# The order of the quantising steps carried on into steps 48 to 55, and one norm's rstd moved ahead on GpSimd

## The reference

```
x = x + tanh(g_xattn[0]) * xattn0(layernorm(x), ctx)
x = x + tanh(g_ffn[0])   * ffn0(layernorm(x))        # MX: fp6 activations, fp4 weights
x = x + tanh(g_xattn[1]) * xattn1(layernorm(x), ctx)
x = x + tanh(g_ffn[1])   * ffn1(layernorm(x))        # int4 weights, a permutation, a bias

xattn: 32 query heads, 8 KV heads of 128; q and k are RMS-normalised per head;
       softmax(q k^T / sqrt(128) + mask) v, then the output projection
ffn0:  mxlinear(silu(mxlinear(x, w_gate)) * mxlinear(x, w_up), w_down)
mxlinear(x, w): both are rounded to a low-bit float in blocks of 32 with a shared exponent
```

## Time and profile before

| | us |
|---|---|
| median of 3 runs | 1346.63 |
| lowest, highest | 1345.92, 1347.79 |
| profiled execution, its own time | 1346.49 |
| its span | 1344.6 |

### The profile page before, as it was taken

The page is one execution under the profiler, slowest core; times in us unless marked ns, Lnnn a source line. Parts: engine busy times, 40 slices in busy tenths (PEclk is TensorE's granted clock), DMA queues, the critical chain, the costliest instruction groups (busy, mean ns, idle before and its releaser), DMA issues.

```text
span 1344.6 us, 25713 instructions
## 1 busy us (share of the span) xinstructions
PE 1336.9 (99%) x7841; PEld 1135.6 (84%) x7841; DVE 960.4 (71%) x1984; ACT 837.0 (62%) x3299; POOL 635.2 (47%) x682
## 2 busy tenths in 40 slices
PE   9999999999999999999999999999999999999999
PEld 7888888888888888777777788888888888888887
DVE  6878787887878798788888857766555555555656
ACT  6767676676767675556656556655666656565542
POOL 3456556564646575356767424432434333332232
PEclk9999999999999999999999999999999999999999
DMA  8011212102121210010100022001010100100001
GB/s 291 1 60 50 67 50 65 52 22 64 49 66 49 67 50 21 1 48 32 49 32 1 1 79 79 32 1 56 32 47 31 45 33 0 47 31 1 2 8 56
DMA packets 32957, 59.49 MB, mean 44 GB/s; under 512 B 2928, under 2 KB 24304, under 8 KB 28784
## 3 DMA queue, kind: packets, MB, share of 16 engines
q1 hardware_dynamic: 32592, 58.01, 13.0%
q10 hardware_dynamic: 288, 0.52, 0.1%
HBM read 56.43 MB, written 2.10 MB: 44 GB/s over the span
## 4 chain that ended last, share of the span: by engine, by line
PE 96%; DVE 1%; POOL 1%; issue 1%; DMA 0%; ACT 0%; SPq 0%; POOLq 0%; DVEq 0%; ACTq 0%
PE bank L1210 66%; PE bank L1202 9%; PE bank L1274 8%; PE bank L1301 7%; PE bank L1236 3%; PE bank L1395 1%; PE bank L1291 1%; PE bank L1407 1%; DMA w_raw<-in_wv 0%; DVE w_lo L823 0%; PE bank L1382 0%; POOL probs L560 0%; POOL rstd L523 0%; DVE probs L1046 0%; POOL f_s L513 0%
## 5 line engine op out<-in xcount | busy, mean ns | idle before, releaser
L494 POOL TENSOR_TENSOR w_lo<-w_raw,w_hi (+1 forms) x150 | 210.7, 1420 | 174.9 <-ACT w_hi L661 174.9
L694 ACT ACTIVATE squares<-bank 128x128 bf16<-128x128 f32 x512 | 134.4, 278 | 196.3 <-PE bank L1210 196.3
L1046 DVE SCALAR_TENSOR_TENSOR probs<-bank,mask_sb 128x512 f32<-128x512 f32 x127 | 87.6, 690 | 205.6 <-PE bank L1274 190.8
L642 ACT ACTIVATE probs<-probs,negmax 128x128 f32<-128x128 f32 x512 | 198.4, 392 | 7.0 <-DVE negmax L929 4.5
L519 POOL TENSOR_TENSOR meansq<-sumsq,scalars 128x5 f32<-128x5 f32 x128 | 28.1, 219 | 359.1 <-ACT squares L694 359.1
L523 POOL TENSOR_TENSOR rstd<-meansq,scalars 128x5 f32<-128x5 f32 x128 | 153.1, 1196 | 10.8 <-POOL meansq L519 1.1
L1210 PE MATMUL bank<-w_hi,oT_hi 128*128 (+1 forms) x512 | 151.1, 417 | 0.0
L1210 PE MATMUL bank<-w_hi,xT_hi 128*128 (+1 forms) x512 | 141.1, 396 | 0.0
L1210 PE MATMUL bank<-w_lo,oT_hi 128*128 (+1 forms) x512 | 138.1, 391 | 0.0
L1210 PE MATMUL bank<-w_hi,oT_lo 128*128 (+1 forms) x512 | 137.9, 391 | 0.0
L1210 PE MATMUL bank<-w_lo,xT_hi 128*128 (+1 forms) x512 | 137.6, 390 | 0.1
(11 more groups left out here) (143 smaller groups left out, 3058.7 us busy)
## 6 DMA issues: line engine op xcount, KB each, us to landing
w_raw<-in_wq SPq DMA_DIRECT2D x16, 1024.0 KB, 4.9
w_raw<-in_wo SPq DMA_DIRECT2D x16, 1024.0 KB, 4.8
fw_raw<-in_ffn_w SPq DMA_DIRECT2D x36, 192.0 KB, 2.3
w_raw<-in_wk SPq DMA_DIRECT2D x16, 256.0 KB, 5.3
w_raw<-in_wv SPq DMA_DIRECT2D x16, 256.0 KB, 5.4
x_sb<-in_x SPq DMA_DIRECT2D x7, 256.0 KB, 9.6
ctx_raw<-in_ctxT SPq DMA_DIRECT2D x7, 256.0 KB, 9.1
fw_raw<-in_ffn_w SPq DMA_DIRECT2D x7, 256.0 KB, 2.7
```

The source lines that it names most:

```text
L494: last = nc.gpsimd.tensor_tensor(lo, raw, hi.bitcast(FP32), ALU.subtract)
L642: last = nc.scalar.activation(probs[:, h * P:(h + 1) * P], probs[:, h * P:(h + 1) * P], ACT.Exp, bias=negmax[:, h:h + 1], accum_out=rowsum ...
L694: last = nc.scalar.activation(squares[:, h // 2, (b + 1) % 4, h % 2, :], q_bank(n, kind)[:, h * P:(h + 1) * P], ACT.Square, scale=SCALE, a ...
L1046: nc.vector.scalar_tensor_tensor(heads(probs[:, :]), heads(psSQ[:, :]), SCALE, mask_sb[:, :].unsqueeze(1).to_broadcast([P, REP, P]), ALU.m ...
```

## The change

A function `calm(n, kind)` is true in QUANT steps and in ZONE steps below 56. Where the order asked for `kind == QUANT`, it now asks for `calm`, on ScalarE, DVE and PE. So steps 48 to 55 take the QUANT order of exponentials, kT, inverse, scores, masked scores and their followers. The place of the weight split isn't touched: it still goes by the kind, on ScalarE (`split_upper`) and GpSimd (`split_lower`). Step 56 has both exponentials now, as step 48 had. On GpSimd, the rstd of the first feed-forward norm (tile 0, in step 56 alone) stands ahead of `unit_rstd`, not behind it.

```diff
+        def calm(n, kind):
+            return kind == QUANT or (kind == ZONE and n < FFN0)
+        def qn_first(n, kind, t):
+            return kind == FIRST or calm(n, kind) or t.down is not None or t.next is not None
...
@@ GpSimd, step
                     split_lower(split_pieces(n, b, kind, j))
+                if t.norm == 0:
+                    ln_rstd_of(NORM["ffn", t.norm])
...
                 if has(n, 0):
                     unit_rstd(n)
...
-                if t.norm is not None:
+                if t.norm is not None and t.norm:
                     ln_rstd_of(NORM["ffn", t.norm])
@@ ScalarE, step
-                exp_late = exp_after(kind) or (kind == FIRST and b == BATCHES - 1)
+                exp_late = calm(n, kind) or (kind == FIRST and b == BATCHES - 1)
...
-                if exp_after(kind) or (kind == ZONE and n == ZONE0):
+                if calm(n, kind) or (kind == ZONE and n == FFN0):
                     softmax_exp(n - 1)
                 if kind in (ZONE, PLAIN):
                     split_upper(split_pieces(n, b, kind, j))
...
-                    if t.active or kind == QUANT:
+                    if t.active or calm(n, kind):
                         layer = layer_of(n, 0, kind)
                         act.wait_ge(kt_ps, n + 1)
                         nc.scalar.activation(kT[:, :], psKV[:, 2 * P:3 * P], ACT.Copy,
@@ VectorE, step
-                    if kind != QUANT:
+                    if not calm(n, kind):
                         row_inverse(n)
...
-                if kind == QUANT:
+                if has(n, 2) and calm(n, kind):
                     row_inverse(n)
...
-                if has(n, 1) and not qn_first(kind, t):
+                if has(n, 1) and not qn_first(n, kind, t):
                     maximum(n)
-                if has(n, 2) and (t.gate is not None or kind == QUANT):
+                if has(n, 2) and (t.gate is not None or calm(n, kind)):
                     probs_lower(n)
                 if has(n, 0) and kind != FIRST:
                     scaled_q(n, kind, t)
...
-                if has(n, 1) and qn_first(kind, t):
+                if has(n, 1) and qn_first(n, kind, t):
                     maximum(n)
...
-                if has(n, 0) and not t.active and kind != QUANT:
+                if has(n, 0) and not t.active and not calm(n, kind):
@@ PE, step
-                if kind == QUANT:
+                if calm(n, kind):
                     scores()
                 if has(n, 2):
                     probabilities()
-                if has(n, 1) and kind != QUANT:
+                if has(n, 1) and not calm(n, kind):
                     scores()
```

More of the change, by code:

```diff
@@ L1054, in step @@
                     scaled_q(n, kind, t)
-                if has(n, 2) and qn_first(kind, t) and kind != QUANT:
+                if has(n, 2) and qn_first(n, kind, t) and not calm(n, kind):
                     probs_lower(n)
-                if has(n, 1) and qn_first(kind, t):
+                if has(n, 1) and qn_first(n, kind, t):
                     maximum(n)
-                if has(n, 2) and t.gate is None and not qn_first(kind, t):
+                if has(n, 2) and t.gate is None and not qn_first(n, kind, t):
                     probs_lower(n)
```

## The result

The changed kernel takes 1349.05 us (median of 19 runs, 1348.70 to 1350.78), the kernel before 1346.78 (19 runs): a ratio of 1.0018, 95% interval 1.0011 to 1.0025. It is slower by 0.18%, or 2.3 us. The forecast was 1349.3 and 0.2%.

The account below looks back on a forecast made before the run. PE was taken to bound the kernel, with a floor of 9.53 us per step without feed-forward work. The terms -0.72 + 5 x 0.82 - 0.67 = +2.7 us gave 1349.3 against the median of 1346.63; range 1344.0 to 1352.0.

Parts of the forecast that it names:

- Step 48: In the new order it takes 9.53 us, like a QUANT step, instead of 10.25: -0.72.
- Steps 49 to 53: Later w_lo on GpSimd holds DVE's scaling, PE's load stalls 1.02: each step 10.55 instead of 9.73, price 0.82.
- Step 57: Earlier rstd brings f_s about 0.9 us earlier, PE's wait goes, the step is as long as step 59: -0.67.
- rival A: New order works as in QUANT steps: steps 49 to 53 fall to 9.53, sum -2.4 us, 1344.2; chance 0.18.
- B: Rival: GpSimd's rstd holds DVE as well in steps 49 to 53, 2.53 each: +11.3 us, 1357.9; chance 0.06.
- C: Rival: stall comes, but step 48's 0.72 turns up in step 56, step 57 gains nothing: +4.1, 1350.7; chance 0.08.

Follow-up runs that it names:

- one w_lo late: Changed kernel with the second w_lo of steps 49, 50, 52 and 53 put last on GpSimd: 1346.20 us, ratio 0.9993.
- the last experiment: Changed kernel with the weight split also in its QUANT place below step 56, first six pieces a step earlier: 1345.10 us, ratio to the kernel before 0.9984.
- the order alone: Changed kernel with GpSimd's rstd of norm 0 back behind the unit's: 1351.35 us, ratio 1.0031.

## Why the prediction was right

**Step 48: right.** -0.72 forecast, -0.72 measured.

**Steps 49 to 53: right in mechanism and nearly in size.** In step 50, counted from its start, forecast and measured: w_hi starts 2.23 and 2.24, v_hi 3.52 and 3.53, the last w_lo ends 5.71 and 5.65, masked scores 7.37 and 7.32, scaled q 8.58 and 8.52, PE's load 9.31 and 9.25, the step 10.55 and 10.44. So the price was 0.71 in four steps, not 0.82. 0.06 of the difference is the shorter pair of w_lo (2.71 in the trace), the other 0.05 lies behind PE's load, where I had let the rest of the step take 1.24 and it takes 1.19. In step 49 the price was 1.17. The piece of step 48 has four blocks, and its last GpSimd instruction ends later:

```profile
472.62 1.05 POOL L537 TENSOR_TENSOR fw_out<-fw_y,blk_pow 128x512 bf16<-128x512 f32 x1
473.70 0.71 DVE L879 STREAM_TRANSPOSE fw_turned<-fw_out 128x512 bf16<-128x512 bf16 x1 [1.66 <-POOL fw_out L537]
...
475.26 2.97 POOL L494 TENSOR_TENSOR w_lo<-w_raw,w_hi 128x512 fp32r<-128x512 f32 x2 [1.60 <-ACT w_hi L663]
...
475.57 1.53 DVE L1019 TENSOR_TENSOR probs<-probs,rinv 128x512 f32<-128x512 f32 x1
```

So DVE came to L1019 0.31 behind w_lo and not 0.36 ahead of it, and was held by it. The second w_lo ended 5.90 into the step instead of 5.65, and it held L857 instead of L860, so that the two 12-column instructions behind L857 were still to come:

```profile
477.23 1.04 DVE L857 TENSOR_SCALAR amax<-amax 128x12 f32<-128x12 f32 x1
```

I had taken the five steps as alike. That DVE came late because of the fourth block is read from the trace, and no run tests it; that the held L1019 costs about 0.48 is what step 49 with one w_lo late shows. The two errors nearly cancel by luck: 3.99 against 4.1.

The forecast read a QUANT step off step 47, which has no piece. Nothing went wrong by it: step 45, which has one of three blocks, also takes 9.53, and step 48 of the changed kernel does too.

**Step 57: right in sign, -0.85 where I took -0.67** as the most there was. I had bounded it by step 59, which takes in a down product's result as well (L999 on DVE); step 57 without its stall is 13.04, shorter than that. Whether that extra work is the 0.18 between them is not shown. The bound was wrong, not the mechanism: L513, L889 and the transposes did what was forecast.

**The time.** The forecast sum was +2.7 and the steps give +2.42: 0.11 less from steps 49 to 53, 0.18 less from step 57. That the medians differ by 2.3 is worth less as support, since the stated range, 1344.0 to 1352.0, took in no change and rival A as well. The positions inside the steps decide.

**Rival A** (-2.4) named what the order could give if nothing collided, and the last experiment shows it (-2.43 in the stretch), with the split moved too. **B** is refuted: in step 50 rstd runs from 489.12 to 490.68, and L866 runs inside it in its usual 0.36. The Trainium skill, "SBUF — State Buffer", section "Who interferes with whom", has whoever issues first, GpSimd or a DVE instruction in a two-port mode, keep the shared pair of ports for the whole instruction. The trace agrees for the 1.28 us of a w_lo. It disagrees for a 5-column rstd, if L866 is in such a mode; no view names the mode. **C** is refuted: step 56 takes 9.52.

## What to carry to other kernels

When a block of instructions is moved to another place in an engine's order, list what else is issued relative to it: here the exponentials moved, w_hi stood behind them, w_lo behind w_hi, and so w_lo began 1.5 us later in the step, on top of the piece's scaling, though no line of GpSimd's in these steps was touched. Where DVE and GpSimd keep each other out, what to look at is where the last long GpSimd instruction ends, against the first DVE instruction of a chain that PE waits for. In steps 50, 52 and 53, leaving one of two there removed the stall, it did not halve it. Two steps that look alike may differ by a block in size, and then a race between two engines that is won in one is lost in the other.

## What the runs showed of the hardware

- A DVE instruction that waits while a GpSimd tensor_tensor of 128x512 runs got its turn between that one and the next, though the next one's input is there (in step 50 both w_hi are through at 486.61, the first w_lo at about 487.64): L857 in steps 50 to 53 of the changed kernel, L1019 in its step 49, L1017 before the change.
- A held 12-column instruction ended 0.02 to 0.04 us behind the end of w_lo, so its own 0.17 is hidden: of the 1.20 us of L860 the chain lost 1.03.
- The start of step 47 differs by up to 2.3 us between the nine profiled executions (452.65 to 454.94), with the same code before it, and the span with it. The scatter lies in the opening. The first matmul of a product (w_hi with ctx_hi) starts 8.21 to 10.47 us into the span, and from there to step 47 it is 444.1 to 444.5 in all nine. In the five that start late (9.75 and more) PE waits 0.5 to 1.5 us there for the first w_lo, which DVE makes; in the four others it doesn't. Behind the stretch, from step 60 on, it is 752.9 to 753.2 in all. Part of this goes by the execution, since executions of one kernel scatter too (the order alone: 1349.88 and 1350.06, then five from 1351.33 to 1351.53). Whether the kernel has a part stays open, since each has one profile. Five medians lie 0.4 to 1.1 us above what their stretches give, and these are the kernels of the five late profiles; in each what the stretch gives lies within the interval of the ratio. Effects of one or two microseconds are read from the stretch, not from the span.
